# Attention in two passes: one for the maximum, one already transposed

## The reference

```
q = (layernorm(x) @ w_q.T + b_q).reshape(B, T, H, D)
k = (ctx @ w_k.T + b_k).reshape(B, S, H, D)
v = (ctx @ w_v.T + b_v).reshape(B, S, H, D)
scores = einsum('bthd,bshd->bhts', q * D**-0.5, k) + attn_bias[None]
scores = where(key_padding_mask[:, None, None, :], NEG_INF, scores)
attn = softmax(scores, axis=-1)
x = x + einsum('bhts,bshd->bthd', attn, v).reshape(B, T, E) @ w_out.T + b_out
x = x + ffn(layernorm(x))        # fp4 round trip on x, w_gate, w_up, h, w_down
```

## Time and profile before

| | |
|---|---|
| median of 3 runs | 1030.16 us (1028.19 to 1031.83) |
| profiled execution | 1029.46 us |
| its span | 1027.5 us |
| TensorE, VectorE, ScalarE, GpSimd busy | 952.6, 857.5, 722.0, 198.6 us |
| mean granted TensorE clock | 0.983 of full speed |
| moved by DMA | 76.14 MB |

### The profile page before, as it was taken

One profiled execution on the slowest core, in us unless ns is written; L12 is line 12 of the kernel. 1 busy time (PEld: TensorE's weight loads), 2 busy tenths in 40 slices (PEclk: granted clock), 3 DMA queues, 4 the chain that ended last, 5 costly groups with the idle time before them and its releaser, 6 DMA issues.

```text
span 1027.5 us, 23032 instructions
## 1 busy us (share of the span) xinstructions
PE 952.6 (93%) x6612; PEld 667.7 (65%) x6612; DVE 857.5 (83%) x2125; ACT 722.0 (70%) x1685; POOL 198.6 (19%) x156
## 2 busy tenths in 40 slices
PE   5299999999999999999999999978778999999997
PEld 3176666666657666665765766645456878878885
DVE  3287988888888888888888878899757999999996
ACT  2298988877888888888788888856634555555542
POOL 3222232140240213114024121245400000000000
PEclk9699999999999999999999999999979999999999
DMA  9553451451533335055153433611000000000000
GB/s 290 134 124 76 113 124 27 121 138 28 120 101 90 84 103 123 15 129 132 36 115 93 103 75 89 145 35 31 2 0 6 17 16 15 21 16 15 20 16 26
DMA packets 47339, 76.14 MB, mean 74 GB/s; under 512 B 10016, under 2 KB 26784, under 8 KB 47264
## 3 DMA queue, kind: packets, MB, share of 16 engines
q1 hardware_dynamic: 47264, 75.34, 29.3%
HBM read 20.78 MB, written 4.19 MB: 24 GB/s over the span
## 4 chain that ended last, share of the span: by engine, by line
PE 82%; DVE 8%; issue 5%; SPq 2%; ACT 2%; DMA 1%; DVEq 1%; POOL 0%; ACTq 0%; POOLq 0%
PE psum L967 24%; PE psum L1099 14%; PE psum L1056 12%; PE psum L1235 9%; PE psum L1217 4%; PE psum L1219 4%; PE psum L1218 4%; PE psum L988 3%; PE psum L995 3%; PE psum L1013 2%; PE psum L982 2%; DVE att L845 2%; DVE att L764 2%; SPq L367 1%; SPq L378 1%
## 5 line engine op out<-in xcount | busy, mean ns | idle before, releaser
L569 ACT ACTIVATE att<-att,neg_max 128x512 f32<-128x512 f32 x512 | 367.3, 719 | 119.1 <-DVE neg_max L845 111.9
L845 DVE CUSTOM_DVE_ANT_0 att<-psum,att 128x512 f32<-128x512 f32 x512 | 346.7, 686 | 106.2 <-PE psum L1099 94.2
L967 PE MATMUL psum<-ident,att 128*128 128x128 f32 x2448 | 364.7, 275 | 19.9 <-DVE att L764 7.4
L967 PEld LDWEIGHTS psum<-ident,att 128*128 128x128 f32 x2448 | 298.0, 141 | 94.6 <-issue 45.6
L1099 PE MATMUL psum<-stack 128*128 128x512 f32 x512 | 273.1, 535 | 26.4 <-DMA stack<-kl 17.3
L1099 PEld LDWEIGHTS psum<-stack 128*128 128x128 f32 x512 | 96.7, 189 | 141.4 <-DVE neg_max L845 81.3
L764 DVE COPY att<-psum 128x512 f32<-128x512 f32 x256 | 175.6, 686 | 3.7 <-PE psum L967 3.7
L1056 PE MATMUL psum<-att 128*32 128x256 f32 x2048 | 164.0, 393 | 2.0 <-issue 2.0
L608 ACT ACTIVATE att<-psum 128x512 f32<-128x512 f32 x256 | 150.5, 588 | 18.1 <-PE psum L967 13.1
L1235 PE MATMUL psum<-att 128*128 128x256 f32 (+1 forms) x384 | 98.0, 388 | 2.8 <-ACT att L649 2.8
L569 ACT ACTIVATION_READ_ACCUMULATOR att<-att,neg_max 128x1 f32 x512 | 96.9, 189 | 0.0
(11 more groups left out here) (96 smaller groups left out, 1043.7 us busy)
## 6 DMA issues: line engine op xcount, KB each, us to landing
stack<-qh SPq DMA_DIRECT2D x128, 128.0 KB, 2.4
stack<-ql SPq DMA_DIRECT2D x128, 128.0 KB, 2.3
att<-in_fside_1xSxS_dram SPq DMA_DIRECT2D x16, 512.0 KB, 3.7
stack<-kh SPq DMA_DIRECT2D x128, 64.0 KB, 2.0
stack<-kl SPq DMA_DIRECT2D x128, 64.0 KB, 2.0
att<-in_ctx_dram SPq DMA_DIRECT2D x8, 512.0 KB, 4.8
out_dram<-att SPq DMA_DIRECT2D x32, 128.0 KB, 1.7
x<-in_x_dram SPq DMA_DIRECT2D x1, 3584.0 KB, 20.4
```

What stands on the lines that cost most here:

```text
L569: act.activation(prob[:, slot, :], prob[:, slot, :], ACT.Exp, bias=neg_max[:, slot:slot + 1], scale=-1.0, accum_out=row_sum[:, o, tt * 8 + ...
L845: dve.tensor_tensor_reduce(out=prob[:, slot, :], in0=ps_score[:, bank_of(j)[0], :], in1=bias_m[:, tt, :], scale=-1.0, scalar=BIG, op0=ALU. ...
L967: return pe.transpose(out_, in_, ident[:, :])
```

## The change

Attention goes over the scores twice. The first pass makes the scores [t, s] as before, but keeps only the row's minimum of the negated sum; the full result goes to a scratch tile `waste`. The second pass makes them transposed, [s, t], straight on top of the transposed and masked bias, which ScalarE or VectorE has copied into PSUM before (a seed). The maxima are a further part of the contraction: they are split in two, transposed, and put by DMA into two rows of q_stack, against rows of ones in k_stack. One exp over two heads' tiles (1024 elements) writes the layout that the value matmuls need. The values have a column of ones, so the row sum comes out of the value matmul, and no accumulator and no transpose of probabilities is left. The two heads of a unit lie in partitions 0 to 63 and 64 to 127, with 48 rows (first pass) or 50 (second) in use.

A period of eight heads has 16 steps. Step s has two tiles of the first pass and one unit of the second, which runs 12 steps behind (LAG), so that the second pass of a period's first half begins at step 12 of it and that of its second half at step 4 of the next. SEED_BY says which engine seeds each of a half's eight units.

By the loops of the diff, stack_q and stack_k issue 12 DMAs of 16 partitions each for each half of a period, stack_m 16 DMAs of two partitions for each half. The rest of attention (outputs normalised in [t, d] layout, transposed back, projected) has its order rewritten to fit. The feed-forward steps themselves are the same.

```diff
-    TILES = 32
-    UNIT = 8
+    N_OCT = 2 * B
+    STEPS, LAG = 16, 12
+    TILES = 2 * STEPS
+    QSTEPS = 8
+    UNITS = N_OCT * STEPS
+    SEED_BY = "AADAAADA"
...
+            def stack_q(m, slot, h):
+                for part in range(2):
+                    wait(sp, (q_high, q_low)[part], m + 1)
+                    plain(sp)
+                    for kk in range(2):
+                        for r in range(2):
+                            head = slice(64 * h + 32 * kk + 16 * r, 64 * h + 32 * kk + 16 * r + 16)
+                            for i in ((0, 1), (2,))[part]:
+                                rows = slice(64 * r + 16 * i, 64 * r + 16 * i + 16)
+                                sp.dma_start(q_stack[rows, slot, kk, :].bitcast(F32), (qh, ql)[part][head, :].bitcast(F32)).then_inc(stacked[slot], 16)
+            def stack_k(m, slot, h):
+                ...                     # the same with kh, kl; parts (0, 2) and (1,)
+            def stack_m(quad, slot):
+                sp.wait_ge(mT_taken, quad + 1)
                 plain(sp)
+                for r in range(2):
+                    for kk in range(2):
+                        for tt in range(NT):
+                            row = 16 * r + 8 * kk + 2 * tt
+                            sp.dma_start(q_stack[64 * r + 48:64 * r + 50, slot, kk, tt * P:(tt + 1) * P].bitcast(F32),
+                                         m_row[row:row + 2, :].bitcast(F32)).then_inc(m_stacked, 16)
+            sp.wait_ge(ones_ready, 1)
+            for h in range(2):
+                stack_q(0, h, h)
+                stack_k(0, h, h)
+            def period(b, o):
+                first, last = is_first(b), is_last(b)
+                n = 2 * b + o
+                if o == 0 and not last:
+                    ...                 # context and mask of the next batch
+                if not (first and o == 0):
+                    stack_m(2 * n - 1, 2 * (1 - o) + 1)
+                if o == 1 and last:
+                    sp.wait_ge(tx_ready, 2 * B)
+                    sp.wait_ge(tc_ready, 2 * B)
                     weights_in(range(4))
+                if o == 0 or not last:
+                    wait(sp, st_ready, 16 * n - 8)
+                    plain(sp)
+                    stack_q(n + 1, 2 * (1 - o), 0)
+                if o == 0:
+                    stack_k(n + 1, 2 * (1 - o), 0)
+                stack_m(2 * n, 2 * o)
+                if o == 1 and not last:
+                    stack_k(n + 1, 2 * (1 - o), 0)
+                if o == 0 or not last:
+                    wait(sp, st_ready, 16 * n)
+                    plain(sp)
+                    stack_q(n + 1, 2 * (1 - o) + 1, 1)
+                    stack_k(n + 1, 2 * (1 - o) + 1, 1)
+                if o == 1 and not last:
+                    for tt in range(NT):
+                        sp.wait_ge(biased, n * TILES + 2 * (QSTEPS + 2 * tt + 2))
                         plain(sp)
+                        sp.dma_start(bias_m[:, tt, :], bias_v[:, tt, :]).then_inc(bias_in[tt], 16)
...
             batches(sp, body)
+            stack_m(2 * N_OCT - 1, 3)
+            weights_in(range(4, PIECES))
...
+            def exp_unit(n, s):
+                m, h, bu = unit_of(n, s)
+                c, kk = bu // 2, bu % 2
+                U = STEPS * n + s - LAG
+                act.wait_ge(st_ready, U + 1)
+                ...
+                act.activation(probT[:, c % 2, 2 * kk:2 * kk + 2, :], pair_of(s), ACT.Exp).then_inc(exp_ready, 1)
+            def seed_unit(n, s):
+                ...
+                act.activation(pair_of(s), bias_mT[:, c, :].unsqueeze(1).to_broadcast([P, 2, S]), ACT.Copy).then_inc(seeded_act, 1)
...
+            def split_m(quad, h):
+                dve.wait_ge(biased, 16 * (quad + 1))
+                wait(dve, mT_ready, quad)
+                dve.tensor_copy(m_hl[:, :, 0], nm[:, h, :]).then_inc(m_high, 1)
+                dve.wait_ge(m_high, quad + 1)
+                dve.tensor_tensor(m_hl[:, :, 1], nm[:, h, :], m_hl[:, :, 0].bitcast(F32), ALU.subtract).then_inc(m_split, 1)
+            def take_mT(quad):
+                dve.wait_ge(mT_ready, quad + 1)
+                wait(dve, m_stacked, 256 * quad)
+                dve.tensor_copy(m_row[:, :], ps_misc[0:32, 0:P]).then_inc(mT_taken, 1)
...
+                        dve.tensor_tensor_reduce(out=waste[:, r, :], in0=ps_A[:, r, :], in1=bias_m[:, tt, :], scale=-1.0,
+                                                 scalar=BIG, op0=ALU.add, op1=ALU.min,
+                                                 accum_out=nm[:, h, col:col + 1]).then_inc(biased, 1)
...
+                            if s == 1 and not (first and o == 0):
+                                take_mT(2 * n - 1)
+                            if s == 9:
+                                take_mT(2 * n)
...
+                            if o == 0 and s == 5:
+                                high_q(n + 1, 1, 384 * (b + 1))
+                    if s == 7:
+                        split_m(2 * n, 0)
+                    if s == 15:
+                        split_m(2 * n + 1, 1)
...                                     # high_k: o == 0 at s == 6, o == 1 at s == 11; high_q: o == 1 at s == 1
+            def scores(n, o, s, r):
+                h, tt, kk, t = s // QSTEPS, (s % QSTEPS) // 2, s % 2, n * TILES + 2 * s + r
+                wait(pe, biased, t - 1)
+                rows = slice(64 * r, 64 * r + 48)
+                pe.matmul(ps_A[:, r, :], q_stack[rows, 2 * o + h, kk, tt * P:(tt + 1) * P], k_stack[rows, 2 * o + h, kk, :],
+                          start=True, stop=True).then_inc(score_ready, 1)
+            def unit(n, o, s, r):
+                ...
+                    if bu == 0:
+                        pe.wait_ge(m_stacked, 256 * (2 * m + h + 1))
+                    by = SEED_BY[bu]
+                    pe.wait_ge(seeded_act if by == "A" else seeded_dve, seeds(2 * m + h, bu, by))
+                rows = slice(64 * r, 64 * r + 50)
+                last = pe.matmul(ps_B[:, 2 * (s % 2) + r, :], k_stack[rows, slot, kk, c * P:(c + 1) * P], q_stack[rows, slot, kk, :],
+                                 start=False, stop=True, skip_group_check=True)
+            def values(m, o, h, c):
+                ...
+                for j in range(4):
+                    last = pe.matmul(ps_O[32 * j:32 * j + 32, :], vpad[:, o, c, 4 * h + j, :], probT[:, c % 2, j, :],
+                                     start=c == 0, stop=c == SC - 1)
...
+                for s in range(STEPS):
+                    if s % QSTEPS == 0:
+                        pe.wait_ge(stacked[2 * o + s // QSTEPS], 384 * (b + 1))
+                    has_b = not (first and o == 0 and s < LAG)
+                    scores(n, o, s, 0)
+                    if has_b:
+                        unit(n, o, s, 1)
+                        unit(n, o, s, 0)
+                    scores(n, o, s, 1)
+                    if has_b:
+                        rounds(n, o, s)
```

More of the change, by code:

```diff
@@ new lines, in body @@
+            def body(b):
+                first = is_first(b)
+                for o in range(2):
+                    n = 2 * b + o
+                    for s in range(STEPS):
+                        place["batch_of"] = lambda t, s=s, o=o: (b if (o == 1 or t >= LAG or t < s) else b - 1)
+                        step(b, o, n, s, not (first and o == 0 and s < LAG), not (first and o == 0 and s < LAG - 1))
+            batches(act, body)
+            for s in range(LAG):
+                step(None, 0, N_OCT, s, True, s + 1 < LAG)
+                if s == 2:
+                    take_oT(N_OCT - 2, 0, ps_misc)
@@ L1047, in _, with weights_free @@
[L1047 to L1059 removed]
+            def weights_free(q):
+                pe.wait_ge(gwT_taken, q + 1)
+                pe.wait_ge(gw_low, min(q + 1, IC))
@@ L1063, in _ @@
+            for i in range(2):
+                make_tc(0, i, psum[:, 5 + i, :])
             pe.wait_ge(w_in_sem, 16)
```

1039 lines of the change are left out of this document (573 added, 466 removed).

## The result

The changed kernel takes 1421.56 us in the median of four runs (1415.92 to 1428.6), against 1029.18 us for the kernel before on the same chip (1027.6 to 1031.83). The ratio is 1.3812, with a 95% interval of 1.3743 to 1.3882: 392 us slower. I had forecast 1250 us, in a range of 1100 to 1310, so the direction held and the size did not.

The account below looks back on a forecast made before the run. The sync engine's queue, 160 stacking issues a batch, and the loop through stack_m were to bound attention: 112.7 us a batch against 85.8. Feed-forward starting at 966.0 plus its 281.5 gives a 1247.5 us span, forecast 1250, range 1100 to 1310.

Parts of the forecast that it names:

- What bounded the kernel before: Attention before the change: TensorE sets the pace, busy 84.7 of 86.0 us in one batch.
- The step: Attention's engines alone allow 2.2 us a step, 2.3 with one more switch: 36.8 us a period against 42.9.
- second rival: All stacking issues at 0.62 us: 1285 us; with steps of 3.0 us besides, 1356; chance above 1300: 0.06.
- The engine sums: Work per attention step: TensorE 2.2 us, ScalarE 1.9 us, VectorE 1.9 us.
- The bias loads: Sync queue, end of the odd period: four bias loads instead of two, at 0.42 us each.
- The price of a two-row issue: Each two-row DMA of stack_m taken at 0.55 us, between ends of 0.37 and 0.62.
- The loop through stack_m: Maxima need 8.9 us to issue, 2.0 to land; TensorE waits about 5; at least 24.3 between stack_m.
- The sum: Whole kernel: start and six batches of 112.7 reach 828.0 us, last even period 882.0, feed-forward start 966.0, span end 1247.5.
- The first (issue at 0.37): Two-row DMAs of stack_m issue at 0.37 us: 101.1 us a batch, 1157 us in all; chance 0.22.
- the third (back-pressure): Stacking's 590 ns is back-pressure of 32 rows, small DMAs issue faster; at 0.2 us about 930 us; chance 0.07.
- The signs: If right: 1280 stacking issues, TensorE's q_stack waits 5 us and more, clock below 0.95, batch about 113 us.
- The clock: In the stack_m loop, 1.0 us added for TensorE's low clock, granted 0.68 and 0.74 behind an idle stretch.

Follow-up runs that it names:

- a_free_first: Changed kernel with bias loads on ScalarE's queue, most stacking left out (stale operands), ps_misc reads put before each step's exp and first maximum pass: 1026.65 us.
- t_both: Changed kernel with stack_m in 4 DMAs, bias loads on ScalarE's queue, stack_k on GpSimd's, ps_misc reads before exp and first maximum pass: 1030.05 us.
- a_first: Changed kernel, its DMAs and queues kept, with only ScalarE's and VectorE's ps_misc reads moved before the step's exp and first maximum pass: 1305.46 us.
- b_price: Kernel before, with series of SBUF-to-SBUF DMAs of various sizes added behind its last output row on three queues: 1081.59 us.
- t_both_r: The same kernel as t_both, run again in five rounds: 1026.24 us, ratio 0.9963 to the kernel before.
- t_sp: Changed kernel with stack_m in 4 DMAs, bias loads on ScalarE's queue, ps_misc reads first, all stacking on the sync queue: 1092.49 us.
- a_bias: Changed kernel with only the next batch's four bias loads issued by ScalarE instead of the sync queue: 1379.65 us.
- a_free_bias: Changed kernel with bias loads on ScalarE's queue and most stacking left out (stale operands), order as written: 1251.88 us.

## Why the prediction was wrong, by its own steps

**What bounded the kernel before**, and the batch of 85.8 us: nothing that I measured speaks against it.

**The step.** This is the term that failed: "with one more switch I take 2.3 us". Wrong was to take the largest engine sum for the step, and to put the hand-overs of ps_misc at nothing. A step measured 3.1 us in the changed kernel between a landing and the next maxima, and 3.6 on the mean with the queue left out; with both copies first it is 2.6. So 1.0 us a step is the written order. The other 0.3 was missed too: with no queue to speak of and the order mended, a_free_first still takes 1026.65 us, and the win of some 100 us that I expected from the engines alone is not there. I had put 3.0 into my second rival ("every switch and hand-over paid in turn") as an end of a range, but had not read in the diff who stands ahead of each reader of ps_misc, which would have shown that it must be paid in nearly every step.

The engine sums agree with the eight free steps: TensorE 2.26 for 2.2, VectorE and ScalarE 1.93 and 1.96 (15.45 and 15.66 over eight) for 1.9. For TensorE that is in part luck. From the starts in t_both's timeline, scores with their switch take 0.91 a step (1.04 forecast), since the two halves of the rows run beside each other, which I had not taken; half a value group takes 0.50 (0.57); and the side work takes 0.89 (0.59), the eight steps holding more of it than the mean.

**The bias loads.** I priced four of them by their issue time, at the queue's end, and nothing by who waits for them. The queue's end in an odd period was forecast 34.4 us after the second stack_m's start; it came 37 us after it, and the next stack_m came at 41.9, because TensorE had stood still for 15 us before it made those maxima. Taking the loads away from there brought 42 us with stack_m in 16 DMAs and 80 with it in four.

**The price of a two-row issue**: 0.55 taken, 0.61 measured, within its bounds and worth 0.96 us on each stack_m.

**The loop through stack_m** is there as forecast: 9.71 of issue, 2.0 to land, and from one stack_m to the next 28.1 us where no q and k are late (24.3 forecast; 0.8 of the difference is the issue, the rest the step). TensorE waited 95.2 us for it in 30 waits: 3.2 each where I had said 5, because it arrived later.

**The sum**, term by term. The second half of the second period's maxima are issued at 164.3 (151.8 forecast); six batches of 132.9 (112.7) bring it to 961.5; the last even period is 60.9 (54.0), the tail up to the feed-forward stage 106.5 (84.0), and that stage 285.2 (281.5). The differences, 12.5 + 121.0 + 6.9 + 22.5 + 3.7, are 166.6 us: 1247.5 becomes the measured span of 1414.1.

What a batch's 20 us are made of is seen from one stack_m to the next, beside a_first (stack_m at 474.33, 513.27, 542.00, 567.23 and 593.08), which differs from the changed kernel in the order alone:

| from one stack_m to the next, us | forecast | changed kernel | a_first |
|---|---|---|---|
| even period, first to second | 29.7 | 34.0 | 28.7 |
| to the odd period's first | 24.3 | 29.0 | 25.2 |
| odd period, first to second | 24.3 | 28.1 | 25.9 |
| to the next batch | 34.4 | 41.9 | 38.9 |
| batch | 112.7 | 133.0 | 118.8 |

With the copies first, three of the four intervals are within 1.6 us of the forecast: the queue and its loop were sized about right, and the step was not. The order is worth 14.2 of the 20.3 us, and 116 us of the whole kernel. In the fourth interval the bias wait is left. In the tail, the two last stack_m end 72.8 us after the last odd period's first began (57.5 forecast), and the weights behind them take 33.7 us (26.5).

**The rivals.** The first (issue at 0.37) and the third (back-pressure) fall by b_price. The third rested on a rule of the Trainium skill, DMA: Bandwidth & Descriptors, Issuing engines are not separate DMA queues: that the sequencer's time is usually small relative to the DMA itself. For one DMA that holds here too (0.6 of issue against 2.0 of landing); for 80 in one queue it does not, since landings overlap and issues don't: 49 us a period, and t_both_r against t_sp shows 66 us for moving 24 of them. The second, all at 0.62 with steps of 3.0, gave 125.6 a batch and 1356 us. It was the nearest, short by the bias wait: a_bias, without that wait, has 126.1 a batch (and 1379.65 us, the rest lying at the two ends). I gave everything above 1300 a chance of 0.06.

**The signs.** The 1280 stacking issues at their price, the low clock and the waits into q_stack were right, though a wait was 3.2 us and not 5. The batch of 113 us was not (133), and the last sign, "a step well over 2.3 us between two stack_m waits would show the engine sum wrong though the total may be near", is the one that came. That the chain of waits would be mostly the sync engine's can't be read: the chain on the page accounts for a quarter of the span only.

**The clock.** I gave it 1.0 us a stack_m. Granted was 0.77 over a batch, and TensorE's busy time 85.7 us, against 72 at the pace of the eight free steps (18.04 x 4): 14 us a batch. It came with the waits and went with them, since the same work in t_both_r has 0.90 and 75.7. No run holds the clock still while the order changes, so what part of the order's gain is the clock's own stays open; a_free_bias and a_free_first bound it by the 14.3 us of busy time in 33.1.

## What to carry to other kernels

Where a change makes a buffer be handed round once a step, the sum of the largest engine is a floor, not the step (2.3 us here, 2.6 reached at best, 3.6 as written): write down for each reader of the shared bank what stands ahead of it on its engine and what waits behind, and put the copies out of it first. Price a DMA in a long queue by everything that is issued behind it and by who waits for that, not by its own issue. When two limits lie in one loop, measure each fix with the other one in place and taken away: the same 24 issues were worth 13 us, if anything, beside a bad order and 66 beside a good one.

## What the runs showed of the hardware

- The issue of a DMA from SBUF to SBUF by the sync engine took 0.60 to 0.67 us for 2 to 128 rows of 512 bytes to 4 KB, on ScalarE's queue 0.64 and on GpSimd's 0.50 (b_price, start to start).
- Two matmuls over 48 and 50 rows in different halves of the partitions run beside each other: L1218 and L1232 both start at 498.24, and the first ends after 0.50 us. The Trainium skill, TensorEngine Tiling (Array Packing), Key Properties, says that tiles operate independently; these rows agree.
- The granted clock can fall behind short waits. In t_both_r TensorE was busy 11.3 of the 12 us from 421 to 433, with one wait of 0.47 us before 432.45. A value group took 1.06 us at 430.49 and 1.93 at 435.24. The clock stayed at the lower level while TensorE waited, and also from 443 to 447, where it was busy throughout; then it came back (stage table, columns as the earlier trace rows):

```profile
435.00:439.00 4.00, 3.94 (x14) 1.20 (x13) 2.22 (x10) 1.34 (x3) 4.00 (x10) 0.50 0.87 265
439.00:443.00 4.00, 1.80 (x6) 0.81 (x7) 1.59 (x5) 2.72 (x3) 3.98 (x6) 0.50 0.39 99
443.00:447.00 4.00, 4.00 (x16) 1.49 (x16) 3.24 (x9) 2.05 (x2) 3.56 (x4) 0.50 0.02 3
447.00:451.00 4.00, 4.00 (x20) 1.53 (x19) 2.87 (x8) 2.78 (x4) 0.00 (x0) 0.91 0.01 1
```

- VectorE's copy of 1024 elements from SBUF to PSUM took 1222 ns, ScalarE's 1028 (the changed kernel, L896 and L668).
